# A fused cross-attention kernel: denominators of the last unit from the exponentials themselves, turns of feature parts with key parts, large early loads kept off ticks 24 to 29

## What is computed

```python
# layer 0: 16 heads of 32
Q = x @ Wq.T + bq;  K = ctx @ Wk.T + bk;  V = ctx @ Wv.T + bv      # per head
att = softmax(Q K^T / sqrt(32));  out = (att V) @ Wo.T + bo
x1 = layernorm(out + x) * gamma0 + beta0
# layer 1: linear attention with elu as feature map
Q_phi, K_phi = elu(x1), elu(ctx)
KV = K_phi^T ctx;  Z = 1 / (Q_phi . sum(K_phi) + 1e-6)
result = layernorm(x1 + (Q_phi KV) * Z) * gamma1 + beta1
```

## Time and profile before

| | |
|---|---|
| time, median of 3 runs | 1528.52 us (1524.69 to 1529.03) |
| the profiled execution | 1526.61 us |
| its span, first to last instruction | 1525.2 us |
| mean granted TensorE clock | 0.988 |
| TensorE busy (matmul) | 1481.1 us, 97% |
| VectorE busy | 1297.9 us, 85% |
| GpSimd busy | 1237.8 us, 81% |
| ScalarE busy | 826.7 us, 54% |
| DMA over the span | 112 GB/s |

### The profile page before, as it was taken

How to read it: one execution, slowest core, us unless ns; L and a number is a source line. 1 busy time by engine, 2 the same in 40 slices (tenths; PEclk the granted TensorE clock), 3 DMA queues, 4 the chain that set the end, 5 groups by cost and what they waited for, 6 DMA issues and landing times.

```text
span 1525.2 us, 30133 instructions
## 1 busy us (share of the span) xinstructions
PE 1481.1 (97%) x10528; PEld 1043.0 (68%) x10528; DVE 1297.9 (85%) x2509; ACT 826.7 (54%) x1595; POOL 1237.8 (81%) x1100
## 2 busy tenths in 40 slices
PE   8999999999999999999999999999999999999886
PEld 6767767676767777667676767666767667756554
DVE  6687888778898988987898897989789889988886
ACT  2454655555555555665555555655555555555542
POOL 0486787767899898967888898877889898897995
PEclk9999999999999999999999999999999999999998
DMA  7744254433325244243344326235242434410001
GB/s 223 212 134 135 70 161 128 148 110 111 111 85 149 79 130 148 77 127 120 96 126 128 104 85 179 91 101 141 87 130 86 145 112 116 130 51 27 7 22 42
DMA packets 159574, 170.14 MB, mean 112 GB/s; under 512 B 20288, under 2 KB 122048, under 8 KB 159424
## 3 DMA queue, kind: packets, MB, share of 16 engines
q1 hardware_dynamic: 157696, 167.16, 36.7%
q10 hardware_dynamic: 1728, 1.05, 0.2%
HBM read 125.97 MB, written 42.21 MB: 110 GB/s over the span
## 4 chain that ended last, share of the span: by engine, by line
PE 83%; DVE 5%; POOL 5%; issue 3%; DMA 2%; ACT 1%; SPq 1%; POOLq 0%; DVEq 0%; ACTq 0%
PE score L465 15%; PE scoreT L479 14%; PE acc L497 13%; PE misc L540 7%; PE misc L552 7%; PE misc L516 7%; PE misc L529 7%; PE misc L577 6%; PE misc L569 4%; POOL pair_sum L1044 2%; PE acc L506 2%; DVE maxes L778 1%; DVE pair_sum L818 1%; POOL pair_sum L1053 1%; PE misc L560 1%
## 5 line engine op out<-in xcount | busy, mean ns | idle before, releaser
L643 ACT ACTIVATE p_ring<-scoreT 128x512 f32<-128x512 f32 x1024 | 597.6, 595 | 552.2 <-PE scoreT L479 546.3
L1044 POOL TENSOR_TENSOR pair_sum<-p_ring 128x512 f32<-128x512 f32 x512 | 665.5, 1308 | 173.1 <-ACT p_ring L643 106.9
L778 DVE TENSOR_REDUCE maxes<-score 128x1 f32<-128x512 f32 x1024 | 678.8, 678 | 114.9 <-PE score L465 108.7
L465 PE MATMUL score<-k_stack,q_stack 96*128 96x512 f32 x1024 | 601.9, 589 | 6.8 <-DVE maxes L778 5.1
L479 PEld LDWEIGHTS scoreT<-q_stack,k_stack 104*128 104x128 f32 x2048 | 390.0, 192 | 155.9 <-ACT p_ring L643 80.1
L479 PE MATMUL scoreT<-q_stack,k_stack 104*128 104x256 f32 x2048 | 421.9, 288 | 7.1 <-ACT p_ring L643 6.6
L465 PEld LDWEIGHTS score<-k_stack,q_stack 96*128 96x128 f32 x1024 | 193.5, 189 | 164.4 <-issue 101.5
L1053 POOL TENSOR_TENSOR pair_sum<-pair_sum 128x512 f32<-128x512 f32 x192 | 253.3, 1319 | 0.0
L497 PE MATMUL acc<-p_ring,v_sb 128*32 128x256 f32 x4096 | 250.1, 385 | 0.0
L818 DVE TENSOR_TENSOR pair_sum<-pair_sum 128x512 f32<-128x512 f32 x192 | 216.7, 1129 | 5.8 <-POOL pair_sum L1044 5.8
L497 PEld LDWEIGHTS acc<-p_ring,v_sb 128*32 128x32 f32 x4096 | 120.8, 110 | 85.4 <-issue 3.5
(11 more groups left out here) (95 smaller groups left out, 1361.8 us busy)
## 6 DMA issues: line engine op xcount, KB each, us to landing
xT_sb<-xT_in SPq DMA_DIRECT2D x63, 512.0 KB, 3.9
q_stack<-q_dram SPq DMA_DIRECT2D x189, 128.0 KB, 2.5
k_stack<-k_dram SPq DMA_DIRECT2D x93, 256.0 KB, 4.4
ctx_nat<-ctx_in SPq DMA_DIRECT2D x32, 256.0 KB, 4.2
q_dram<-q_high SPq DMA_DIRECT2D x63, 128.0 KB, 1.7
q_dram<-q_low SPq DMA_DIRECT2D x63, 128.0 KB, 1.9
k_dram<-k_high SPq DMA_DIRECT2D x31, 256.0 KB, 2.0
k_dram<-k_low SPq DMA_DIRECT2D x31, 256.0 KB, 2.2
```

What stands on the lines that cost most here:

```text
L465: pe.matmul(score[k % 3][:], q_stack[0:SPLIT, unit % NQ, j, t * P:(t + 1) * P], k_stack[0:SPLIT, group_of[unit] % 2 * QUAD + j, h * HALF:( ...
L643: act.activation(p_ring[:, n % NP, h * HALF:(h + 1) * HALF], scoreT[k % 2][:], ACT.Exp, scale=SCALE).then_inc(A["exped"], 1)
L778: dve.reduce_max(maxes[:, unit % 2, t, j, h:h + 1], score[k % 3][:], AX.X).then_inc(V["maxed"], 1)
L1044: pool.tensor_tensor(pair_sum[:, place_of_pair(pair), cols], p_ring[:, (n - 1) % NP, cols], p_ring[:, n % NP, cols], ALU.add).then_inc(L[" ...
```

## The change

Three edits.

1. For the last unit (63, `unit >= SUMMED`) the pair sums and running sums on GpSimd and VectorE are left out. In each of its two visits TensorE multiplies the four tiles of exponentials with ones too, into `acc[:, 256:512]`, and the matmuls on the sum are left out. VectorE's turn waits for `weighted` in place of `divided`, and ScalarE's exponentials no longer wait for pair sums that aren't made. The planner books nothing for them.
2. For tiles 24 to 31 the parts of phi alternate between `phiT_high`, `phiT_low` (even) and `k_high`, `k_low` (odd). The planner lets T of tiles 25 to 31 follow A of two tiles before, and ScalarE's copy waits accordingly; for tile 25 it waits until the last key parts have been put.
3. Bulk transfers are kept off ticks 13 to 29 in place of 13 to 23.

```diff
+    SUMMED = UNITS - 1
...
-        phiT_high = sb("phiT_high", [P, D], F32R)
-        phiT_low = sb("phiT_low", [P, D], F32R)
+        phiT_high = [sb("phiT_high", [P, D], F32R), k_high]
+        phiT_low = [sb("phiT_low", [P, D], F32R), k_low]
...
+        def place_of_phiT(tile):
+
+            return tile % 2 if tile >= TILES - KT else 0
...
-            while k in steps or room["SP"].get(k, 0) + transfers > 3 or bulk and (k >= UT and 2 <= k % UT < 8 or 13 <= k < UT + 8):
+            while k in steps or room["SP"].get(k, 0) + transfers > 3 or bulk and (k >= UT and 2 <= k % UT < 8 or 13 <= k < UT + 14):
...
-            if k // 2 % 2 == 0:
+            if k // 2 % 2 == 0 and k < UT * SUMMED:
                 take("POOL", k + LEAD + 4, 13)
-            if k % 4 == 0 and k % UT > 0:
+            if k % 4 == 0 and k % UT > 0 and k < UT * SUMMED:
                 take("POOL", k + LEAD + 6, 13)
                 take("DVE", k + LEAD + 7, 10)
...
-                         "T": [("O", i, 0), ("A", i - 1, 0)],
+                         "T": [("O", i, 0), ("A", i - (2 if i > TILES - KT else 1), 0)],
...
+                if unit >= SUMMED:
+                    for s in range(VISIT):
+                        n = VISIT * v + s
+                        for j in range(QUAD):
+                            mm = pe.matmul(acc[j * DK:(j + 1) * DK, CH:2 * CH], ones[:, 0:DK],
+                                           p_ring[:, n % NP, j * CH:(j + 1) * CH], start=False,
+                                           stop=n % KT == KT - 1, tile_position=(0, j * DK), skip_group_check=True)
                 mm.then_inc(T["weighted"], 1)
-                if part < KT // VISIT - 1:
+                if unit >= SUMMED or part < KT // VISIT - 1:
                     return
...
-                    act.wait_ge(L["paired"], 2 * ((n - NP) // 2 + 1))
+                    if n - NP < KT * SUMMED:
+                        act.wait_ge(L["paired"], 2 * ((n - NP) // 2 + 1))
...
-                if tile > 0:
-                    act.wait_ge(T["attended"], tile)
-                act.activation(phiT_high[:], bank_of("T", tile)[:], ACT.Copy).then_inc(A["phiT_high_kept"], 1)
+                if tile == TILES - KT + 1:
+                    act.wait_ge(M["k_out1"], landed_keys(GROUPS - 1, 1, 2))
+                elif tile > 0:
+                    act.wait_ge(T["attended"], tile - (tile > TILES - KT))
+                act.activation(phiT_high[place_of_phiT(tile)][:], bank_of("T", tile)[:], ACT.Copy).then_inc(A["phiT_high_kept"], 1)
...
-                    dve.wait_ge(T["divided"], unit + 1)
+                    if unit < SUMMED:
+                        dve.wait_ge(T["divided"], unit + 1)
+                    else:
+                        dve.wait_ge(T["weighted"], KT // VISIT * (unit + 1))
...
-                if 0 <= unit < UNITS and p > 0 and i == 0:
+                if 0 <= unit < SUMMED and p > 0 and i == 0:
                     add_high(unit, p)
...
-                if 0 <= pair < KT * UNITS // 2 and i < 2:
+                if 0 <= pair < RUN_PAIRS * SUMMED and i < 2:
                     add_pair(pair, i)
                 unit, p = divmod(pair, RUN_PAIRS)
-                if 0 <= unit < UNITS and p > 0 and i == 2:
+                if 0 <= unit < SUMMED and p > 0 and i == 2:
                     add_low(unit, p)
```

More of the change, by code:

```diff
@@ L568, in attend @@
                 for term, (phiT, kv) in enumerate(((phiT_high, kv_high), (phiT_high, kv_low), (phiT_low, kv_high))):
-                    mm = pe.matmul(bank_of("A", tile)[:], phiT[:, d * P:(d + 1) * P], kv[:, d, :],
+                    mm = pe.matmul(bank_of("A", tile)[:], phiT[place_of_phiT(tile)][:, d * P:(d + 1) * P], kv[:, d, :],
                                    start=d == 0 and term == 0, stop=d == G - 1 and term == 2)
@@ L941, in keep_phiT_low @@
                 dve.wait_ge(A["phiT_high_kept"], tile + 1)
-                dve.tensor_tensor(phiT_low[:], bank_of("T", tile)[:], phiT_high[:].bitcast(F32),
+                place = place_of_phiT(tile)
+                dve.tensor_tensor(phiT_low[place][:], bank_of("T", tile)[:], phiT_high[place][:].bitcast(F32),
                                   ALU.subtract).then_inc(V["phiT_low_kept"], 1)
```

## The result

The changed kernel takes 1524.27 us in the median of 13 runs (1519.80 to 1526.92), the kernel before 1527.38 in 13 runs (1523.80 to 1529.18): ratio 0.9976, 95% interval 0.9966 to 0.9986. It is faster, but by 3 to 4 us (3.1 by the medians, 3.7 by the ratio) where I had forecast 10. The profiled execution took 1522.6 us, with a span of 1521.3 and a mean clock of 0.993.

The account below looks back on a forecast made before the run. TensorE was taken as the bound, busy 1481 of 1525 us. From the profiled 1526.61, -3.9 -1.5 -5.4 +0.7 gave 1516.5, plus 1.9 for the runs' median 1518.4; 8-in-10 range 1512 to 1525.5.

Parts of the forecast that it names:

- Denominators: Last unit: dropping the sums ends TensorE's 5.34 us wait and the slow clock behind it; 5.4 us gained.
- Rival 2: At the end VectorE becomes the bound or the clock stays down; only 2.5 of 5.4 stays, 1521.3 us; 15%.
- rival 3: Last unit's ones: weight loads stand in line, 7.0 us more at the end, 1525.4 us; 3%.
- Key put stall: 50 to 55 us: key puts land early, TensorE's hole and slow clock go, queries wait 0.3; net 3.9 us gained.
- Context: Near 77 us: xT(6) moves behind the context loads, shortening the second hole; 1.5 us gained, between 0 and 2.9.
- T31 in front of A30: At the end: A30 starts 2.2 us later, its norm and the last store up to 1; 0.7 us lost.
- A31 ends where it did: At the end: although A30 starts 2.2 us later, A31's end isn't moved; lower bound of the loss nothing.
- The median: Whole kernel: three runs' median lies 1.9 us above the profiled execution, so 1516.5 becomes 1518.4.
- the two early steps: Early stage: 3.9 us from the first hole near 52 us and 1.5 from the context hole near 77.
- queries late: At tick 32 the wait for unit 2's queries replaces the removed one, context hole stays; 1523.8 us; 17%.

Follow-up runs that it names:

- e2: Kernel before with only the last unit's denominators taken from the exponentials by TensorE: 1520.10 us, ratio 0.9964.
- e4: Changed kernel with tile 31 alone planned by the old rule, so that T31 follows A30: 1520.99 us, ratio 0.9961.
- e3: Kernel before with only the feature parts taking turns, so that T31 stands in front of A30: 1529.17 us, ratio 1.0009.
- e9: Changed kernel with six matmul calls that compute nothing needed, filling TensorE's wait ahead of T31: 1521.72 us, ratio 0.9968.
- e1: Kernel before with only the wider ban on bulk transfers: 1525.88 us, ratio 0.9989.
- e7: Changed kernel with T31 behind A30, context loads from tick 54, stacking of keys 2 and 3 not before tick 39: 1520.01 us, ratio 0.9953.
- e10: As e7, with three matmuls that compute nothing needed ahead of each of T30, A30 and A31: 1517.58 us, ratio 0.9931.
- e5: Changed kernel with the stacking of keys 2 and 3 not before tick 39: 1523.83 us, ratio 0.9983.
- e6: As e4, with the context loads planned from tick 54 instead of 36: 1521.32 us, ratio 0.9960.
- e8: Changed kernel with only the put of unit 1's maxima issued by ScalarE instead of SP: 1523.58 us, ratio 0.9980.
- g1: Kernel before once more, unchanged, for a second look at its trace: 1525.98 us, one execution.

## Why the prediction was right and wrong

- Denominators, 5.4 forecast: right in size. 5.5 by e2's ratio, 6.4 by its median; 5.9 at O30. All its pieces came: visit with ones 3.84 us, A28 at full clock (2.8 us instead of 5.3), VectorE's turn at 1484.66. What the step left out: the 1.0 to 1.6 us that the end then loses in e2 and e4, with A30 partly at half clock. Rival 2, that VectorE takes the place of the wait, didn't come.
- Loads of weights in line (rival 3): 32 ones' matmuls took 1.91 us beside 32 loads of 110 ns, 3.5 us in line. The Trainium skill's rule (TensorE: Matmul & The Clock Gate, The mechanism) that loads overlap only where the row group differs isn't what this trace shows: all have the same rows. The same section of the Trainium skill also names a background weight buffer as a target that lets a load go ahead; no row here tells whether that is what happens.
- Key put stall, 3.9 forecast. This step of the prediction failed most: "Net: 3.9 gained" charged the wait for the queries alone. The chain of events was right: the two puts at once, the stall of ScalarE gone, the queries last, at 47.11 in place of the 47.8 worked out. Three sizes failed. The gain was read off one execution with a hole of 2.68 and a fallen clock; two of four had 1.6 and full clock; the mean over four traces fell by 1.0 us. The wait for the queries was 0.9 to 1.7 us, not 0.3. And the step stopped at the first wait: it asked what is late at tick 32, but not what the train, pushed from ticks 24 to 29 into 31 to 33, would stand in front of. Key stacks and loads are 2.5 MB (512 KB + 2 x 256 + 6 x 256) issued between 48.6 and 54.1; unit 1's put comes at 55.6, and at the 256 GB/s of 50 to 55 us the train is some 10 us of transfer, under way until 58.5 at the earliest; the rows have it under way until 61. Before, the put went out at 60.9, when little of the traffic was left, and landed in 2.8. That cost 1.1 to 2.6 us, named in no rival.
- Context, 1.5 forecast: near in size. The prediction read its 1.52 off one trace; the four traces of the early order as before have 1.52 to 3.14 us there, 2.6 in the mean, the four as changed 0.89 to 2.05, 1.3 in the mean. So 1.3 us less wait, with a spread nearly as large, and the clock behind it comes on top (0.86 in 75 to 80 us before, 1.00 in the changed kernel).
- T31 in front of A30, 0.7 forecast, 2.3 to 3.3 measured (changed against e4, by ratio and by median; 2.2 in the traces), 1.4 alone in e3. The delay of A30 was right: 4.72 us behind T30 for 2.34 in e4, 2.4 later, 2.2 forecast. The step failed at "A31 ends where it did": it took A30 at full clock. It ran at half clock, 5.16 us for 2.83, ended 3.1 us later than in e4 (9.88 against 6.74 us behind T30), and the norm of tile 30, behind which tile 31's root stands on GpSimd, passed that on to the end (20.5 against 18.3). Of the 3.1 us, 2.4 are the later start and 0.8 the clock beyond what e4's A30 lost too; only 2.2 reached the end. Even at full clock 0.7 was too little: e9 ran A30 at full clock but 3.6 us later behind T30 than the kernel before (5.98 for 2.34) and ended 2.7 later, so by that measure a start 2.4 later costs 1.5 (an estimate). I had the numbers for the clock: I had charged it behind the waits at 52 and at 1486, and not behind this one.
- The median: I added 1.9 us for the profiled execution's distance from three runs. With 13 runs that distance is 0.8.

In sum: 5.4 + 5.4 - 0.7 was forecast (denominators, the two early steps, T31). By the ratios 5.5 came for the denominators (e2), -2.3 for T31 (changed against e4), and 0.5 for the early loads as what is left of 3.7; e1, the loads alone, gave 1.7. Either is far below 5.4, but how the early loss divides between waits and clock is known only from traces that vary by more than that. Of the rivals, "queries late" (1523.8) is nearest in number but not in cause: the wait that took the old one's place was for the maxima.

## What to carry to other kernels

When large transfers are moved off one place, list every small transfer that will then be issued within the next microseconds behind them, down to the 16 KB ones, and charge each wait with its landing at the stretch's bandwidth; moving them once more only helps when nothing late stands behind the new place either. Where an engine's wait is charged with a fallen clock at one place, weigh it at all like places (the same waits ahead of A30 came with a full clock in before and with half in e7), and in a tail made of waits of 1 to 2 us try to fill them: harmless matmuls gave 1.3 us in the traces' end here and 2.4 in the medians. Take the size of a stall from several executions before it carries half of a forecast.

## What the runs showed of the hardware

- One early order of instructions gave first holes of 1.59, 1.67, 2.68 and 3.00 us in four executions, with a granted clock in 50 to 55 us of 1.00, 1.00, 0.66 and 0.69: the low clock went with the long holes. Of e7 and e10, with the same early order and the same wait of 0.42 us near 74.7, the first had a clock of 0.66 in 75 to 80 us and the second 1.00. The Trainium skill (TensorE: Matmul & The Clock Gate, What's actually happening) says that the gate runs free of the kernel, so that slow matmuls vary from run to run; e7 and e10 agree.

```profile
75.00:80.00 5.00, 4.73 (x28) 2.83 (x30) 4.66 (x11) 2.39 (x4) 3.85 (x4) 0.66 0.48 139
75.00:80.00 5.00, 4.45 (x44) 2.67 (x43) 4.87 (x11) 2.39 (x4) 3.84 (x4) 1.00 0.50 147
```

- A put of 16 KB landed in 1.9 us with little in front (e5, e7) and behind 2.5 MB in 6.2 to 7.8 us from SP's queue (e1, e9, e6, changed, e4) and in 6.4 from ScalarE's (e8).
- The clock fell to half in A30 behind waits of only 1.5 and 1.7 us, with 0.6 us of work between them, and did not when they were filled but for 0.24 and 0.42 us (e7 and e10). It did not fall there in before, g1 and e1 either, with the same two waits but half clock at A28, some 20 us earlier.
- A matmul call of two 32-bit operands that aren't marked fp32r ran as two instructions of 0.44 us for 512 columns at full clock (e9: six calls, twelve instructions, 5.32 us); those of A30, fp32r, are one instruction each, 0.23 to 0.24 us apart (e10: twelve in 2.83 us).
